# Loading x in three places, count one-hots in two halves, and the experts' second product with 512 moving columns

## What is computed

```python
def _gcn_norm(edge_index, num_nodes):
    ...
    deg = jax.ops.segment_sum(ones, dst, num_segments=num_nodes)
    dis = jnp.where(deg > 0, jax.lax.rsqrt(deg), 0.0)
    norm = dis[src] * dis[dst]
...
def _gcn_layer(x, src, dst, norm, W, b, num_nodes):
    xw = x @ W
    msg = xw[src] * norm[:, None]
    out = jax.ops.segment_sum(msg, dst, num_segments=num_nodes)
    return out + b
...
    # experts: xn is the normalized token, per expert e scaled by ln_g and ln_b
    h = jax.nn.gelu(jnp.einsum('end,edh->enh', xe, W1) + b1[:, None, :], approximate=False)
    y = jnp.einsum('enh,ehd->end', h, W2) + b2[:, None, :]
    ...
    out = (weights[:, :, None] * sel).sum(axis=1)
...
edge_index = jnp.stack([src, dst])
xn = _layernorm(x, axis=-1)
x = x + _L0_gnn_ref(xn, edge_index, ...) + _L0_mix_ref(xn[None], ...)[0]
x = x + _L0_ffn_ref(_layernorm(x, axis=-1)[None], ...)[0]
```

## Time and profile before

| | us |
|---|---|
| median of three runs | 3344.09 |
| lowest, highest | 3339.18, 3347.6 |
| the profiled execution | 3348.99 |
| its span, first to last instruction | 3346.7 |
| mean granted clock of TensorE | 0.817 |

### The profile page before, as it was taken

The page is one execution under the profiler, slowest core; times in us unless marked ns, Lnnn a source line. Parts: engine busy times, 40 slices in busy tenths (PEclk is TensorE's granted clock), DMA queues, the critical chain, the costliest instruction groups (busy, mean ns, idle before and its releaser), DMA issues. The chain is left out here.

```text
span 3346.7 us, 47049 instructions
## 1 busy us (share of the span) xinstructions
PE 2393.5 (72%) x11743; PEld 1816.8 (54%) x11743; DVE 1734.3 (52%) x4351; ACT 620.0 (19%) x1318; POOL 1994.5 (60%) x2107
## 2 busy tenths in 40 slices
PE   3376676666777768366666666666769399999998
PEld 2144444444444446244344444444448199999998
DVE  6144444444444456244444445554556766666665
ACT  1000000000000005000001010101116344444443
POOL 1576766666666653766666666666743055555554
PEclk9777888888777789666767778777779599999999
DMA  6433332333333322444444444444422455555551
GB/s 150 131 94 90 91 92 87 90 91 90 88 90 92 88 77 82 120 137 143 144 137 146 146 136 146 146 147 146 146 73 77 158 180 147 146 147 149 147 147 20
DMA packets 178034, 397.68 MB, mean 119 GB/s; under 512 B 42398, under 2 KB 96575, under 8 KB 169644
## 3 DMA queue, kind: packets, MB, share of 16 engines
q0 software_dynamic: 96800, 233.29, 26.1%
q1 hardware_dynamic: 46516, 99.22, 8.2%
q10 hardware_dynamic: 34552, 63.24, 5.8%
HBM read 323.27 MB, written 75.01 MB: 119 GB/s over the span
## 5 line engine op out<-in xcount | busy, mean ns | idle before, releaser
L628 POOL DMA_INDIRECT rows<-rows_layer,srcs x1564 | 1550.8, 992 | 751.8 <-issue 394.3
L689 PE MATMUL l_bank<-rows,sel 128*128 x3332 | 1207.3, 493 | 639.7 <-issue 246.1
L679 DVE TENSOR_TENSOR acc<-acc,l_bank 128x256 f32 x1666 | 699.5, 420 | 1234.9 <-remote 493.7
L689 PEld LDWEIGHTS l_bank<-rows,sel 128*128 128x128 f32 x3332 | 710.2, 238 | 1012.3 <-issue 468.8
L657 DVE TENSOR_TENSOR sel<-iota_n,dloc 128x512 f32<-128x512 f32 x418 | 286.5, 686 | 20.1 <-issue 20.1
L1574 POOL DMA_INDIRECT out<-ys,g_sum x112 | 180.9, 1615 | 190.0 <-DVE ys L1530 164.8
L1491 ACT ACTIVATE hr<-ffn_bank,vec 128x256 f32<-128x256 f32 x448 | 213.0, 475 | 385.4 <-PE ffn_bank L1432 362.0
L1430 PE MATMUL ffn_bank<-wh,hhi 128*128 128x256 f32 x896 | 257.6, 288 | 0.0
L1430 PE MATMUL ffn_bank<-xh,wh 128*128 128x256 f32 x896 | 252.3, 282 | 2.4 <-DVE xl L1506 2.4
L1432 PE MATMUL ffn_bank<-wh,hlo 128*128 128x256 f32 x896 | 253.1, 282 | 0.0
L1432 PE MATMUL ffn_bank<-xh,wl 128*128 128x256 f32 x896 | 251.9, 281 | 0.0
(11 more groups left out here) (274 smaller groups left out, 2319.6 us busy)
## 6 DMA issues: line engine op xcount, KB each, us to landing
wh<-w_hi SPq DMA_DIRECT2D x32, 1024.0 KB
wl<-w_lo SPq DMA_DIRECT2D x32, 1024.0 KB
rows<-rows_layer,srcs POOLq DMA_INDIRECT x1564
w_qkv<-wide ACTq DMA_DIRECT2D x49, 335.0 KB
w_hi<-whi ACTq DMA_DIRECT2D x49, 335.0 KB
w_lo<-wlo ACTq DMA_DIRECT2D x49, 335.0 KB
rows_layer<-acc SPq DMA_DIRECT2D x25, 256.0 KB, 2.1
rows_x<-acc SPq DMA_DIRECT2D x7, 910.0 KB
```

The lines of the kernel that those rows point to most:

```text
L628: pool.indirect_dma_start(rows[:, (n + 1) % ROWS, :], None, table[layer], bass.IndirectOffsetOnAxis(ap=srcs[:, n:n + 1], axis=0)).then_inc ...
L679: v.tensor_tensor(to, to, step_bank(s), ALU.add).wait_op(sem(f"summed{layer}"), s + 1, "sem-ge").then_inc(sem(f"added{layer}"), 1)
L689: t.matmul(step_bank(s), sel[:, s % SELS, :], rows_flat[:, bass.ds(slot * D, D)], start=True, stop=True).wait_op(sem(f"here{layer}"), t.to ...
```

## The change

Three edits in one kernel.

- **Loading.** `s_pm` is loaded by POOL inside the branch for edges out of order, and SP no longer waits for it. Chunk 0 of x is loaded by ACT in block "order" once `d_pm` is there, chunk 1 by ACT at the start of block "prep", and chunks 2 to 6 and the last rows by SP, after it has waited for `rows_d`.
- **One-hots.** Each one-hot is written in two halves, first columns 0 to 103 of all four quarters of the 832 steps, for all 36 values, then columns 104 to 207. TensorE starts its first 104 matmuls after 36 of the 72 instructions.
- **Second product.** `wh` and `wl` become two planes of one tile, `whl`. One matmul with weights `hh` streams both planes, 512 columns, into two halves of a bank, and a second with weights `hl` streams `wh`, 256 columns. `ps_y` is two banks now, and VectorE sums the two halves with one more operation; `e_yb` counts two a tile.

```diff
@@ def load_x
+        def load_x(eng, c):
+
+            n = XCH - (c == XIN - 1)
+            eng.dma_start(node[:, c * XCH:c * XCH + n, :],
+                          x[c * XCH * P:(c * XCH + n) * P, :].rearrange("(t p) d -> p t d", p=P)).then_inc(sem(f"x_in{c}"), 16)
@@ block "order"
-                    sp.dma_start(s_pm[:, :], src.rearrange("(p w) -> p w", w=SP_W)).then_inc(sem("spm"), 16)
-                    sp.wait_ge(sem("spm"), 16)
+
+                @block.scalar
+                def _(a):
+                    a.wait_ge(sem("dpm"), 16)
+                    load_x(a, 0)
...
                     with pool.If(unordered > 0):
+                        pool.dma_start(s_pm[:, :], src.rearrange("(p w) -> p w", w=SP_W)).then_inc(sem("spm"), 16)
@@ block "prep", sync
+                    sp.wait_ge(sem("rows_d"), SG * 16)
+                    for c in range(2, XIN):
+                        load_x(sp, c)
+                    sp.wait_ge(sem("tail0"), 1)
+                    sp.dma_start(node[0:TAIL, NT - 1, :], x[(NT - 1) * P:N, :]).then_inc(sem("x_last"), 16)
                     sp.wait_ge(sem("word_d"), 48)
@@ block "prep", vector
+                    def by_half(ap, lo):
+                        return ap.rearrange("p (q r) -> p q r", r=GP)[:, :, lo:lo + GP // 2]
+
                     v.wait_ge(sem("hi_b"), 1)
-                    for h in range(HI):
-                        v.tensor_scalar(hi_hot[:, h, :], hi_b[:, :], float(h), None, ALU.is_equal).then_inc(sem("hots"), 1)
                     v.wait_ge(sem("lo_b"), 1)
-                    for l in range(LO):
-                        v.tensor_scalar(lo_hot[:, l, :], lo_b[:, :], float(l), None, ALU.is_equal).then_inc(sem("hots"), 1)
+                    for lo in (0, GP // 2):
+                        for h in range(HI):
+                            v.tensor_scalar(by_half(hi_hot[:, h, :], lo), by_half(hi_b[:, :], lo), float(h), None, ALU.is_equal
+                                            ).then_inc(sem("hots"), 1)
+                        for l in range(LO):
+                            v.tensor_scalar(by_half(lo_hot[:, l, :], lo), by_half(lo_b[:, :], lo), float(l), None, ALU.is_equal
+                                            ).then_inc(sem("hots"), 1)
@@ block "prep", tensor
-                    t.wait_ge(sem("hots"), LO + HI)
                     for p in range(GP):
+                        if p % (GP // 2) == 0:
+                            t.wait_ge(sem("hots"), (LO + HI) * (p // (GP // 2) + 1))
@@ block "prep", scalar
-                    for c in range(XIN):
...
-                    a.wait_ge(sem("tail0"), 1)
-                    a.dma_start(node[0:TAIL, NT - 1, :], x[(NT - 1) * P:N, :]).then_inc(sem("x_last"), 16)
+                    load_x(a, 1)
@@ experts
-            wh = [sb(ph, f"wh{i}", [P, WIDE], F32R) for i in range(2)]
-            wl = [sb(ph, f"wl{i}", [P, WIDE], F32R) for i in range(2)]
+            whl = [sb(ph, f"whl{i}", [P, 2, WIDE], F32R) for i in range(2)]
+            wh, wl = [w[:, 0, :] for w in whl], [w[:, 1, :] for w in whl]
...
-            bk = banks(ph, 6)
-            ps_x, ps_h, ps_y = bk[0], bk[1:5], bk[5]
+            bk = banks(ph, 5)
+            ps_x, ps_h = bk[0], bk[1:5]
+            ps_y = ph.enter_context(nc.psum_tensor("ps_y", [P, 2, 2, D], F32))
@@ experts, vector
-                        v.tensor_tensor(ys[q][:, :, :], ps_y[:, :].rearrange("p (h d) -> p h d", h=2),
+                        v.tensor_tensor(ys[q][:, :, :], ps_y[:, :, 0, :],
                                         vec[q][:, None, O_B2:O_B2 + D].to_broadcast([P, 2, D]), ALU.add
                                         ).then_inc(sem("e_yb"), 1)
-                        v.wait_ge(sem("e_yb"), n + 1)
+                        v.wait_ge(sem("e_yb"), n * 2 + 1)
+                        v.tensor_tensor(ys[q][:, :, :], ys[q][:, :, :], ps_y[:, :, 1, :], ALU.add).then_inc(sem("e_yb"), 1)
+                        v.wait_ge(sem("e_yb"), n * 2 + 2)
@@ experts, tensor
                                 at = slice(O_W2 + m * D, O_W2 + (m + 1) * D)
-                                ins = three(t, ps_y[:, h * D:(h + 1) * D],
-                                            (hh[q][:, m, h * P:(h + 1) * P], hl[q][:, m, h * P:(h + 1) * P]),
-                                            (wh[q][:, at], wl[q][:, at]), m == 0, m == HC - 1)
+                                t.matmul(ps_y[:, h, :, :], hh[q][:, m, h * P:(h + 1) * P], whl[q][:, :, at],
+                                         start=(m == 0), stop=False)
+                                ins = t.matmul(ps_y[:, h, 0, :], hl[q][:, m, h * P:(h + 1) * P], wh[q][:, at],
+                                               start=False, stop=(m == HC - 1))
```

12 lines of the change are left out of this document (4 added, 8 removed).

## The result

The changed kernel takes **3334.81 us** (median of 6 runs, 3329.87 to 3338.05) and the kernel before, on the same chip, 3344.51 us (median of 6, 3339.18 to 3351.41). The ratio is 0.9964 with a 95% interval from 0.9953 to 0.9974: faster by 9.7 us, 0.36%. The forecast was 3309.6 us, in a range from 3297 to 3324; the sign was right, the size was not, and the time lies outside the range. 34.5 us had been worked out, and 10.9 came (the profiled execution took 3338.05 us for 3348.99).

A forecast was written before the change was run, and what follows sets the result against it. TensorE was taken to bound the experts, a chain through several engines the start. Experts -21.7 and start -12.8 sum to -34.5 us: 3314.5 against the profiled execution, 3309.6 at the median; range 3297 to 3324.

The forecast's parts named there:

- the term of 25 ns a group: Experts' second product: a group takes 335 instead of 360 ns, 22.4 us saved over 896 groups.
- Where the columns are clearly longer than a load, the surplus is 2.5 ns: Experts' second product: from fp32 rows, a step of 512 columns takes 213 + 3 = 216 ns.
- The 256 step beside the new one: Experts' second product: the remaining step of 256 columns stays at 119 ns, with the next group's load behind it.
- VectorE's splits: Experts' tiles: despite the added sum, splits end at 8.37 us, before TensorE needs them at 8.42; costed at nothing.
- Block at 12.0 us: Start: without the 6.3 us wait for s_pm, the next block begins at 12.0 us instead of 16.1.
- Data 4 us behind the last gather: Start: gathered rows arrive 4 us after the last gather, instead of 12.9, at 27.5 us instead of 40.5.
- Rival 2: Start gains only 4 us: branch or fetch replaces s_pm's wait, and step-word packets hold the gathers; 3318 us, chance 0.12.
- VectorE's stop as a fetch held up behind x: Start: VectorE's stop until 29.00 us is a delayed instruction fetch; without it 14 statistics end at about 24.
- x on SyncE: Start: chunks 2 to 6 arrive by 48 to 56 us, hidden behind VectorE's work; 2 us if that cover is gone.
- halves: Start: half one-hots take 0.18 us each, 13.0 us instead of 10.4, and are worth nothing (+0.2 us).
- VectorE last: Start: VectorE, not TensorE, ends the counts' stage, at 59.1 us against 71.9; TensorE is through at 54.9.
- rival 1: Experts' second product: the 13 ns belong to every instruction, so it saves only 11.6 us; 3320 us, chance 0.15.

The follow-up runs named there:

- The s_pm run: Kernel before, with only the load of s_pm and its wait taken out of the first block: 3338.53 us (one run) beside 3343.40.
- experiment 3: Changed kernel with the three stores of the step words moved behind SyncE's wait for the gathered rows: 3335.68 us (one run).
- experiment 10: Changed kernel with step-word stores behind SyncE's x loads: ratio 0.9943 to the kernel before; second kernel, also VectorE's first statistics before its wait for tile counts: 0.9943.
- the fourth and fifth group: Last two of five sets of runs, each timed beside the kernel before on one chip; that kernel took 3046 and 3051 us there.
- experiment 12: The kernel before run once more, unchanged: 3051.92 us beside 3051.27.

## Why the prediction was wrong

**Experts, the term of 25 ns a group: wrong, and it is where most of the miss sits (15 of 24 us).** The step that failed is "Where the columns are clearly longer than a load, the surplus is 2.5 ns". It was read from the fp32 entries of L814 and carried to fp32r. For fp32 it is right (215.9 ns for two passes of 256) and for bf16 as well (215.8). An fp32r step of 512 takes 233.3 ns, 17.5 above that. The old 256 step's surplus of 13 ns could belong to the weight load or to slower columns, and the prediction gave it to the load; but where columns are few the step is 111 ns, load included, while with 256 fp32r columns it is 117 to 121. The group went from 360.2 to 350.3 ns, under the lower bound of 11.6 us (13 ns a group) with 8.9. Of those 8.9 the tiles keep 6.6 (56 x 0.117 us): the second product is 0.15 us shorter, but in every other tile the first product takes 5.70 us where it took 5.64. Why, no run here shows. The tail gives 0.75 us back, as forecast, which leaves 5.8; that the whole stage comes to -6.6 is luck, since its first tile took 11.0 us now and 12.0 before, and that tile takes 10.6 to 12.0 with the change or without it. The 256 step beside the new one was right (117 against 119), and VectorE's splits were in time.

**Block at 12.0 us: right** (11.44). The s_pm run alone gives these 4.8 us.

**Data 4 us behind the last gather, "near the lower, since what filled the engines is moved behind it": wrong.** It took 11.6 us. What was moved away was x, and what held the gathers was the 2688 small packets. Rival 2 named them, at 0.12; against it stood that x fills the engines. But that the loads of x fill the engines does not mean that they hold the gathers: with all of x and no small packets the data took 4.9 us, with one chunk and no small packets 2.0, with one chunk and the packets 11.6. The Trainium skill (DMA: Bandwidth & Descriptors, Queues, rings and completion order) says that a DMA engine serves its queues by turns, packet by packet; the rows of experiment 3 agree as far as queues beside each other share the engines, and no run tells how it picks, nor why the engines then stand empty for 4 us before the rows count as landed. With the small packets out of the way (the first kernel of experiment 10) the start is 11.3 us shorter than before, near the forecast of 12.8: the rest of the sum for the start held.

**VectorE's stop as a fetch held up behind x: wrong in its cause.** It stays with only the gathers left in the queues (experiment 10: until 24.04 us, with transfers other than theirs over by 18.4), its end follows neither x nor the small packets, and in the last two groups it is absent. It cost nothing in the changed kernel, as the rows came later still; in experiments 3 and 10 it is what keeps VectorE from the rows until 29.4. What it waits for stays open; the trace gives a remote releaser.

**x on SyncE, halves, VectorE last: right.** No wait for x; half a one-hot takes 0.18 us, from one-hots to the second copy it is 27.1 us (38.7 to 65.83) for 27.5 forecast; the halves gain 0.3 us, where they had been forecast to cost 0.2.

**The sum.** The cases were priced apart: rival 1 (3320) and rival 2 (3318) both happened. Together they give -11.6 + 0.7 - 4 = -14.9, 3329 us; the rest up to 3335 is mostly the group, which saved 8.9 and not 11.6, what the first products took back of it, and the scatter of the middle, while the start did 2.2 us better than rival 2. The range ended at 3324, since it held each of them but not both, although no reason tied one to the other or against it: 0.15 x 0.12 looked small, but both were the same kind of error, a gain taken near its better bound.

## What to carry to other kernels

Price a matmul from rows of its own type: merging two fp32r matmuls of 256 columns into one of 512 saves a weight load that was nearly hidden, 10 ns in a group of 360, and not what fp32 or bf16 rows promise. Before moving a large transfer away from an urgent gather, count the packets beside it and not the bytes; a few kilobytes in four-byte packets did more than megabytes of x, and in two of the places that they were moved to, what stood behind them in their queue paid next. And where two parts of a change are each priced near their better bound, let the range reach to the sum of both worse ones.

## What was not expected of the hardware

- fp32r columns are slower than those of fp32 passes and bf16: 233.3 ns against 215.8 for 512, with all else idle and at a granted clock of 1.00. With 128 and with 192 columns the fp32r step is 111 ns; with 128 of bf16 it is 55.9.
- Three stores of 10.5 KB in all, in packets of four bytes, were over 13 us after their last issue with x ahead of them in their queue (41.6 to 54.9), and in the kernel before 24 us (26.1 to 50.2).
- In the fourth and fifth group the same kernel before took 3046 and 3051 us, 9% less than in the first three. The tiles of the experts are as long as ever (11.83 us) and the start within 5 us; the middle, layer 1 to the experts, is 2267 us for 2568. There VectorE stands 494 us for remote releasers in the one and for none among its main waits in the other, like the stop in the start. The two lines are the accumulation's group of the page (busy, mean ns, idle before and its main releaser), first of the kernel before in its first profile, then in the one of experiment 12. Whether it is the chip or its state, no run here tells.

```profile
L679 DVE TENSOR_TENSOR acc<-acc,l_bank 128x256 f32 x1666 | 699.5, 420 | 1234.9 <-remote 493.7
```

```profile
L679 DVE TENSOR_TENSOR acc<-acc,l_bank 128x256 f32 x1666 | 699.6, 420 | 933.1 <-PE l_bank L689 840.0
```
